# A one-layer token tower on one core: attention and the first expert ordered tile by tile, with seven matmuls of zeros in the norm chains

## The reference

```python
h = tok(weight, x, end_ids)              # embedding, plus a vector set by the next end symbol to the right
h = h + attn(layernorm(h), Wq, Wk, Wv, Wm)
h = h + ffn(layernorm(h), ln_g, ln_b, w_r, b_r, W1, b1, W2, b2)

# attn: 8 heads of 16; scores -(q - k)**2 / 4 with scalar q, k per head; softmax; @ Wm; plus its input
# ffn:  t = layernorm(x) * g + b; logits = t @ w_r.T + b_r; top 2 of 8 experts, softmax over the two
#       expert e: gelu(t @ W1[e] + b1[e]) @ W2[e] + b2[e]      (128 -> 512 -> 128)
#       x + sum of the two chosen experts, each times its gate
```

## Time and profile before

| | |
|---|---|
| median of three runs | 102.84 us (102.8 to 103.25) |
| profiled execution: time, span | 103.02 us, 101.0 us |
| mean granted clock of PE | 0.949 |
| busy share: PE, PEld, DVE, ACT, POOL | 84%, 67%, 57%, 54%, 31% |
| PE instructions in the span | 437 |

### The profile page before, as it was taken

The page is one execution under the profiler, slowest core; times in us unless marked ns, Lnnn a source line. Parts: engine busy times, 40 slices in busy tenths (PEclk is TensorE's granted clock), DMA queues, the critical chain, the costliest instruction groups (busy, mean ns, idle before and its releaser), DMA issues.

```text
span 101.0 us, 1448 instructions
## 1 busy us (share of the span) xinstructions
PE 84.8 (84%) x437; PEld 68.0 (67%) x437; DVE 57.8 (57%) x174; ACT 54.9 (54%) x120; POOL 31.3 (31%) x65
## 2 busy tenths in 40 slices
PE   0065899997998972879999999999999999989940
PEld 0043469665998951857788777777777776779930
DVE  1599999889795664559345050413223138269970
ACT  0746397999987132019725566565646463128850
POOL 6832230399996412400000032505050514000000
PEclk9999999999999999555589999999999999999999
DMA  0589999274000000000000000000000000003774
GB/s 5 61 286 403 334 290 290 59 256 162 10 0 0 0 0 0 0 0 0 6 0 0 0 0 0 0 0 0 0 0 0 6 0 0 0 3 114 301 298 118
DMA packets 8167, 7.59 MB, mean 75 GB/s; under 512 B 1440, under 2 KB 6240, under 8 KB 8032
## 3 DMA queue, kind: packets, MB, share of 16 engines
q1 hardware_dynamic: 7440, 7.41, 23.6%
q10 hardware_dynamic: 720, 0.10, 0.6%
HBM read 5.40 MB, written 2.11 MB: 74 GB/s over the span
## 4 chain that ended last, share of the span: by engine, by line
PE 61%; DVE 16%; ACT 13%; DMA 3%; issue 3%; POOL 1%; DVEq 0%
PE ps L1220 21%; PE ps L1305 7%; PE ps L1209 6%; PE ps L1210 6%; PE ps L1211 6%; ACT prob L544 4%; PE ps L1139 3%; DMA ends_i<-in_end_ids 3%; DVE prob L847 2%; DVE prob L725 2%; ACT prob L555 2%; PE ps L1074 2%; PE ps L1232 1%; ACT hn_t L567 1%; ACT L642 1%
## 5 line engine op out<-in xcount | busy, mean ns | idle before, releaser
L661 ACT ACTIVATE w_f<-ps,ffn_cols 128x384 f32<-128x384 f32 x32 | 18.2, 580 | 16.0 <-PE ps L1211 15.9
L1220 PE MATMUL ps<-w_f 128*128 128x384 f32 x64 | 26.0, 496 | 0.0
L1209 PE MATMUL ps<-hn_hi,w_hi 128*128 128x384 f32 (+2 forms) x35 | 21.6, 616 | 1.4 <-DVE hn_lo L885 1.2
L510 POOL TENSOR_TENSOR acc<-acc,term 128x384 f32<-128x384 f32 x6 | 8.7, 1442 | 34.4 <-DVE term L970 34.4
L970 DVE SCALAR_TENSOR_TENSOR term<-ps,ffn_cols,gate_bc 128x384 f32<-128x384 f32 (+2 forms) x9 | 5.1, 571 | 22.9 <-PE ps L1220 15.9
L1210 PE MATMUL ps<-hn_lo,w_hi 128*128 128x384 f32 (+2 forms) x35 | 12.8, 365 | 0.0
L1211 PE MATMUL ps<-hn_hi,w_lo 128*128 128x384 f32 (+2 forms) x35 | 12.6, 361 | 0.0
L1220 PEld LDWEIGHTS ps<-w_f 128*128 128x128 f32 x64 | 11.9, 193 | 0.9
L1209 PEld LDWEIGHTS ps<-hn_hi,w_hi 128*128 128x128 f32 x35 | 7.8, 222 | 5.8 <-DVE hn_lo L885 1.3
L1210 PEld LDWEIGHTS ps<-hn_lo,w_hi 128*128 128x128 f32 x35 | 7.9, 227 | 3.8 <-issue 0.3
L458 POOL TENSOR_TENSOR w_lo<-w_f,w_hi 128x512 fp32r<-128x512 f32 x8 | 10.0, 1289 | 0.0
(11 more groups left out here) (185 smaller groups left out, 132.2 us busy)
## 6 DMA issues: line engine op xcount, KB each, us to landing
w_f<-in_w SPq DMA_DIRECT2D x4, 512.0 KB, 6.8
w_f<-in_w SPq DMA_DIRECT2D x8, 256.0 KB, 6.9
out_y<-w_f SPq DMA_DIRECT2D x6, 256.0 KB, 2.6
cls_all<-cls_dram SPq DMA_DIRECT2D x1, 1024.0 KB, 4.8
out_y<-w_f SPq DMA_DIRECT2D x4, 128.0 KB, 2.3
wm_sb<-in_wm ACTq DMA_DIRECT2D x1, 64.0 KB, 2.4
emb<-in_weight SPq DMA_DIRECT2D x1, 32.0 KB, 2.8
ffn_cols<-in_ffn_columns ACTq DMA_DIRECT2D x1, 24.0 KB, 5.3
```

What stands on the lines that cost most here:

```text
L510: G.tensor_tensor(acc[:], acc[:], term[:, e % 2], ALU.add).then_inc(acc_ready, 1)
L661: nc.scalar.activation(hid[:, e % 2, f], ps[:, n % 4, 0:ROWS], ACT.Gelu, bias=b1_col[:, e, f:f + 1]).then_inc(gelu_ready, 1)
L1209: M(dst, w1_hi[:, e, c], hn_hi[:, rows], start=True, stop=False)
L1220: M(ps[:, 4 + e % 2, 0:ROWS], w2_f[:, e, f], hid[:, e % 2, f], start=(f == 0), stop=(f == FT - 1)).then_inc(down_done, 1)
```

## The change

The diff does more than its title says.

1. Attention: PE, ACT and DVE lists are put in another order, so that tile 0's `shift`, `exps` and `weighted` come before all scores are done. `residual_base` (u_h0) moves from ACT to POOL.
2. The moments of `residual` are read from PSUM by DVE before ACT's copy, not behind it.
3. Expert 0 leaves the common loop: plain f32 matmuls of 128 columns for each tile (`first_up`), Gelu of 128 columns (`first_gelu`), `first_down`. These stand among the steps of the norm chain, together with `hold`: 3, 1 and 3 matmuls of bf16 zeros of 512 columns. The load of ACT's Gelu table moves ahead of `take_rows(0)`.
4. `down(e, i)` takes the hidden rows as the weights and W2 as the moving operand, four plain f32 matmuls of 128 columns for each tile. The result has the rows on the partitions, so the gate is a scalar for each partition: `gates`, `turn_gates`, `turn_base`, `take_gates`, POOL's sums and the nine transposing matmuls of the end go. DVE does `weigh` and `weigh_bias` for each expert and tile. The gates come from a tanh instead of exp and a division.
5. `make_table` follows the last `weigh` of each tile; b2 comes in by one more DMA, 512 KB, at the end of SP's list of loads.

```diff
+            def first_gelu(i, f):
+
+                act.wait_ge(first_done, i + 1)
+                nc.scalar.activation(hid[:, 0, f, tile(i)], ps[:, FIRST_BANKS[i], f * P:(f + 1) * P], ACT.Gelu,
+                                     bias=b1_col[:, 0, f:f + 1]).then_inc(first_ready, 1)
...
+                    if n == 1:
+
+                        act.wait_ge(gap_ready, 1)
+                        nc.scalar.activation(pair_tanh[:], pair_gap[:], ACT.Tanh).then_inc(tanh_ready, 1)
...
             def residual(i):
                 dve.wait_ge(att_done, i + 1)
-                dve.wait_ge(h1_ready, i + 1)
-                moments(h1[:, i], i, stats3, mv3)
+                V.bn_stats(stats3[:, i], ps[:, att_bank(i), 3 * P:4 * P]).then_inc(mean_read, 1)
+                dve.wait_ge(mean_read, i + 1)
+                step(V.bn_aggr(mv3[:, i], stats3[:, i]))
+                settle()
...
+            for e in range(E - 1):
+                for i in range(NT):
+                    weigh(e, i)
+                for i in range(NT):
+                    weigh_bias(e, i)
+                one_hot(e)
+            for i in range(NT):
+                weigh_bias(E - 1, i)
             one_hot(HOT_STEPS - 1)
...
+            for i in range(NT):
+                weigh(E - 1, i)
+                make_table(i)
...
+            def hold(n):
+
+                for _ in range(n):
+                    M(ps[:, FIRST_BANKS[1]], idle[:, 0:P], idle[:], start=True, stop=True)
...
+                elif m == 0:
+                    pe.wait_ge(first_ready, NT * FT)
+                    pe.wait_ge(acc_step, weigh_step(0, NT - 1))
+                for f in range(FT):
+                    mm = M(ps[:, down_bank(e, i), 0:D], hid[:, e % 2, f, tile(i)], w2_f[:, e, f], start=(f == 0), stop=(f == FT - 1))
+                mm.then_inc(down_done, 1)
...
+                for i in range(NT):
+                    if e > 1:
+                        down(e - 1, i)
+                    elif i == NT - 1:
+                        first_down(i)
+            for i in range(NT):
+                down(E - 1, i)
...
-                pe.wait_ge(table_ready, 2 if g < 7 else 4)
+                pe.wait_ge(table_ready, 4 if g < 4 else 6)
```

More of the change, by code:

```diff
@@ L56, with build @@
 UNITS = NT * PAIRS
-GR = LOW + E
 HT = 2 * B
-def build(nc, x, weight, end_ids, columns, wv, wm, b_r, w1, ffn_columns, w2, out):
+def build(nc, x, weight, end_ids, columns, wv, wm, b_r, w1, ffn_columns, b2, w2, out):
     ctx = ExitStack()
@@ L499, in _ @@
                 roots(i)
[L501 to L513, removed]
+            for e in range(6, E):
+                low_w1(e)
         @block.scalar
@@ L568, in take_rows @@
                                      bias=b_col).then_inc(hnt_ready, 1)
[L570 to L576, removed]
+            for e in range(1, 5):
                 high_w1(e)
@@ L1189, in _, with first_up @@
             weighted(2, 2)
+            turn_rows(0)
+            weighted(2, 3)
+            def first_up(i, f):
+                if f == 0:
+                    pe.wait_ge(hnt_ready, i + 1)
+                    if i == 0:
+                        pe.wait_ge(w1_in[0], 16)
+                        pe.wait_ge(shift_ready, UNITS)
+                    if i == 2:
+                        pe.wait_ge(heads_ready, heads_parts(1))
+                mm = M(ps[:, FIRST_BANKS[i], f * P:(f + 1) * P], w1_f[:, 0, f * P:(f + 1) * P], hn_t[:, tile(i)],
+                       start=True, stop=True)
+                if f == FT - 1:
+                    mm.then_inc(first_done, 1)
@@ new lines, in first_down @@
+            def first_down(i):
+                if i == 0:
+                    pe.wait_ge(w2_in[0], 32)
+                    pe.wait_ge(heads_ready, heads_parts(2))
+                else:
+                    pe.wait_ge(logit_read, i + 1)
+                for f in range(FT):
+                    pe.wait_ge(first_ready, FT * i + f + 1)
+                    mm = M(ps[:, FIRST_DOWN[i], 0:D], hid[:, 0, f, tile(i)], w2_f[:, 0, f], start=(f == 0), stop=(f == FT - 1))
+                mm.then_inc(down_done, 1)
@@ L1195, in _, with up @@
             route(0)
-            output(2)
+            hold(1)
             turn_rows(1)
+            hold(3)
             route(1)
-            def up(e, f, rows=slice(0, ROWS)):
-                k = e * FT + f
-                pe.wait_ge(w1_lo_ready, e + 1)
+            for f in range(FT):
+                first_up(1, f)
+            turn_rows(2)
+            first_down(0)
+            route(2)
+            for f in range(FT):
+                first_up(2, f)
+            first_down(1)
+            def up(e, f):
+                k = (e - 1) * FT + f
+                pe.wait_ge(w1_lo_ready, e)
```

409 lines of the change are left out of this document (183 added, 226 removed).

## The result

The changed kernel takes **98.08 us** (median of 97.55, 97.86, 98.30 and 99.51), beside 102.94 for the kernel before on the same chip: a ratio of **0.951, interval 0.945 to 0.956**; the interval leaves the execution of 99.51 out. The profiled execution took 97.55, with a span of 95.8 (1.75 beside it).

What follows compares the result with a forecast made beforehand. Bounds: attention, norm chains (PE waits, then runs at half pace), a PE-bound loop, and the end. Span 81.5 + 7.51 + 3.95 = 93.0, with 2.02 beside it 95.0, plus 1.7 for a cold y: 96.7 us, range 94.2 to 98.8.

Steps and rivals of the forecast that it cites:

- signs of being wrong: Wrong if `up(1, 0)` starts later than 46, or the last `down` and y lie under 2 us apart.
- The stretch at half pace: The 10.14 us from 40.89 at granted clock 0.50; expected at 1.00, with zeros filling waits, charged nothing, at most 0.6.
- The attention: no gain taken: Up to the end of `weighted(2, 3)`: 35.38 before, 35.3 taken, between 34.5 and 36.3.
- The norm chains: From the attention's end to `up(1, 0)`, claimed to start 4.0 us earlier, at 44.05, bounds 43.2 to 45.2.
- The loop: From `up(1, 0)` to the last `down`: 4.5 us shorter, experts 4.76 each, last `down` ending at 78.7.
- The end: Last `down` to y: VectorE finishes late, wait 2.8 (2.6 if operations overlap), y at 81.5, 0.4 lost.
- The clock at the end: In the empty wait before y the clock more likely than not falls, y starting at 1.2 GHz; 1.7 charged, chance 0.44.
- The rival in which the clock survives: The clock stays up through the wait before y: 95.0 us; clock up throughout had chance 0.33.
- The third table load: A 1.28 us load ahead of the tanh and one behind it, delaying `down(1, 0)` by 1.2 more: 97.9, chance 0.02.
- the charge of 1.7: Time added for y starting at 1.2 GHz after the wait before it, bringing 95.0 to 96.7 us.
- The sum without that charge: Whole kernel with the clock up: span 81.5 + 7.51 + 3.95 = 93.0, plus 2.02 beside it, 95.0.

Runs made afterwards that it cites:

- e2_nohold: Changed kernel with the seven matmuls of zeros left out; 99.28 us.
- e6_both_nohold: Changed kernel, GpSimd's two last low halves ahead of its roots, VectorE's last biases and one-hots done after expert 5, no zeros; 93.65 us, ratio 0.912 to the kernel before.
- e10_best: e6_both_nohold with the edit of e9_resid added; 92.42 us, ratio 0.898 to the kernel before.
- e9_resid: Changed kernel with tile 0's moments behind the third tile's last two shifts on VectorE, and ScalarE's residual behind the last exponential; 97.97 us.
- e8_near: Changed kernel with the turn of tile 1's distances put ahead of `weighted(0, 2)` instead of behind it; 98.16 us.
- e1_lo: Changed kernel with GpSimd's low halves of first weights for experts 6 and 7 ahead of its roots again; 97.07 us.
- e4_early: Changed kernel with three more matmuls of zeros between the second and third scores; 98.74 us.
- e12_again: Changed kernel run again with no edit, for the spread of its executions; 97.90 us.

## Why the prediction was right, and where it was not

96.7 was forecast and 98.08 measured, inside the range and on the right side. But one of the prediction's own signs of being wrong came true: `up(1, 0)` started at 47.04, later than 46. Its steps:

- **The stretch at half pace goes.** Right, but the zeros, which the steps relied on, are not what does it: the clock stays up without them in the norm chains of the profiled executions of e2_nohold, e6_both_nohold and e10_best, and the mean clock is 0.99 or more in all twelve executions of the latter two. They cost 0.17 to 0.18. Which part of the new order keeps TensorE busy enough was not tried.
- **The attention: no gain taken.** This step failed. `weighted(2, 3)` ended at 36.81, beyond the bound of 36.3 and 1.5 after the 35.3 that was taken. e9_resid shows 1.02 of it: the moments of tile 0 wait for the first output, and the last shifts wait behind them. The prediction saw that the order puts the moments ahead, and did not charge VectorE's wait there. For the other 0.5 the early clock is the likely cause: it rose near 21.4 in this execution where it had risen at 20.20, and in e6_both_nohold, where it rose near 19, `weighted(2, 3)` ends at 36.23, 0.58 earlier with the same attention lists. e8_near shows that the turn of tile 1 is not it.
- **The norm chains.** Mis-sized: 8.75 us were laid out from the attention's end to `up(1, 0)`, and 10.23 measured. The missing 1.48 is GpSimd beside VectorE (1.29, e1_lo) and the zeros, which were charged nothing and cost 0.18 (e2_nohold). With neither, e6_both_nohold takes 8.75 there, as laid out. The move of the low halves stood in the change; what they do to VectorE's casts was in no term.
- **The loop.** Right: 34.60 for 34.67, and experts 4.76 apart.
- **The end.** Right in kind: VectorE is last before y. The wait is 2.46, where 2.8 was taken, just under the bound of 2.6.
- **The clock at the end.** Held more likely than not, and charged with 1.7; by their spans it happens in three of ten executions. Where a trace shows it (e4_early, e9_resid, e12_again), y takes 9.03 to 9.17 instead of 7.50 to 7.78, 1.3 to 1.7, so the size was about right. The rival in which the clock survives is what the other seven show.
- **The third table load** is not there: no load stands before the tanh.

So the forecast is close partly by luck, since errors offset each other: the charge of 1.7 that the profiled execution did not pay stands against 2.6 by which y starts later than laid out (84.10 for 81.5). The sum without that charge was 95.0, and the profiled execution, with the clock up through y, took 97.55.

## What to carry to other kernels

Where an operation is moved on GpSimd's queue, read what VectorE does beside it at the new place; in this kernel a cast and a subtraction that stay in SBUF waited for it there, at a cost of 1.29 us. Put work that waits for another engine behind work that is ready, even if it seems to be the start of the next stage. The empty wait of some 2.5 us before y cost the clock in some executions and not in others, so one profile does not decide it. Taking the wait away gained 2.46 here, filling it 0.2.

## What the runs showed of the hardware

The same program met the same wait of 2.45 us with two outcomes: y at 1.00 throughout (7.78) and y at 0.51 for 3.33 us (9.03). The early rise moves too, from near 19 in e6_both_nohold (the first two rows) to near 23 in e12_again (the last two), with the same TensorE instructions up to there. A matmul of the scores has a record of 0.52 at the lower level and of 0.34 at the upper, and lies between where the rise falls into it:

```profile
18.98 0.41 PE L1082 MATMUL ps<-key_side,query_side 128*128 128x384 f32 x1
...
19.59 0.34 PE L1082 MATMUL ps<-key_side,query_side 128*128 128x384 f32 x1
...
22.64 0.52 PE L1098 MATMUL ps<-query_side,key_side 128*128 128x384 f32 x1
22.96 0.39 PE L1081 MATMUL ps<-key_side,query_side 128*128 128x384 f32 x1
```

The first moment moves with it (31.87 to 33.02). The granted clock column says 1.00 in that stretch in both, so a mean clock does not count this time at the lower level. The Trainium skill (TensorE: Matmul & The Clock Gate, "What's actually happening") says that the gate is not in step with the kernel's start, so that the point of change differs by up to 500 ns either way from run to run. These two agree that it moves, but by some 4 us (18.98 to 22.96), and the measurement decides.

In this kernel GpSimd holds up VectorE only in some operations. A cast and a subtraction in SBUF went from 0.22 and 0.29 to 1.31 and 1.26. A subtraction that reads PSUM took 0.54 beside low halves of the same size, and 0.54 without them (33.14 above):

```profile
21.33 6.24 POOL L456 TENSOR_TENSOR w_lo<-w_f,w_hi 128x512 fp32r<-128x512 f32 x5
...
25.31 0.54 DVE L824 TENSOR_TENSOR prob<-prob,ps 128x384 f32<-128x384 f32 x1
```
